# Five tiles of the third path block summed in PSUM instead of four, and two of the second block's tiles scattered at the border of the blocks

## What is computed

```python
x1 = x_nodes[src].reshape(-1, N_SEG, EXTENT)            # 4352 edges, 16 segments of 32
x2 = x_edges.reshape(-1, N_SEG, EXTENT)
i1, i2, i3 = (path_indices[:, 0], path_indices[:, 1], path_indices[:, 2])   # 64 paths
contrib = path_coeffs[None, :, None] * x1[:, i1, :] * x2[:, i2, :]
edge_out = jnp.zeros((x2.shape[0], N_SEG, EXTENT)).at[:, i3, :].add(contrib)
out = jnp.zeros((n_nodes, OP_SIZE)).at[dst].add(edge_out.reshape(-1, OP_SIZE))
```

## Time and profile before

| | |
|---|---|
| median of 3 runs | 277.52 us (277.49 to 278.12) |
| span of the profiled execution, first to last instruction | 276.2 us |
| PE busy | 263.4 us, 95% |
| DVE busy | 224.0 us, 81% |
| ACT busy | 164.3 us, 59% |
| block 2's paths on PE | 188.0 to 227.6 us |

### The profile page before, as it was taken

The page is one execution under the profiler, slowest core; times in us unless marked ns, Lnnn a source line. Parts: engine busy times, 40 slices in busy tenths (PEclk is TensorE's granted clock), DMA queues, the critical chain, the costliest instruction groups (busy, mean ns, idle before and its releaser), DMA issues.

```text
span 276.2 us, 5644 instructions
## 1 busy us (share of the span) xinstructions
PE 263.4 (95%) x1631; PEld 185.6 (67%) x1639; DVE 224.0 (81%) x660; ACT 164.3 (59%) x335; POOL 63.1 (23%) x52
## 2 busy tenths in 40 slices
PE   6899999999999899998999999969999999999996
PEld 4566698886444799996678776746656674468633
DVE  5977565199657999999999999999999987655372
ACT  6920551011526699946879786497898839352260
POOL 4000060060006644304769991000000000000000
PEclk9999999999999999999999999977999999999999
DMA  6699990000014557733150002014445428100002
GB/s 203 232 414 405 447 397 12 0 2 1 1 38 129 177 144 252 233 100 101 53 139 17 2 1 76 4 37 141 148 154 152 154 84 320 54 2 2 2 0 76
DMA packets 12592, 33.91 MB, mean 123 GB/s; under 512 B 3345, under 2 KB 3602, under 8 KB 12306
## 3 DMA queue, kind: packets, MB, share of 16 engines
q1 hardware_dynamic: 10482, 26.73, 27.0%
q0 software_dynamic: 2080, 6.82, 8.4%
HBM read 32.50 MB, written 1.05 MB: 121 GB/s over the span
## 4 chain that ended last, share of the span: by engine, by line
PE 85%; DVE 7%; ACT 3%; issue 2%; POOL 1%; ACTq 0%; DVEq 0%; POOLq 0%
PE psum L1276 16%; PE psum L1327 16%; PE psum L1230 10%; PE psum L1330 8%; PE psum L1254 5%; PE psum L1259 4%; PE psum L1282 3%; PE psum L1401 3%; PE psum L1427 3%; PE psum L1173 3%; PE psum L1159 2%; PE psum L1318 2%; PE psum L1182 1%; PE psum L1439 1%; PE psum L1320 1%
## 5 line engine op out<-in xcount | busy, mean ns | idle before, releaser
L460 POOL DMA_INDIRECT big<-xn_rows,big x26 | 51.4, 1975 | 54.4 <-DMA xn_rows<-xn 23.5
L1276 PE MATMUL psum<-big,dst_oh 128*128 128x512 f32 x108 | 51.3, 601 | 0.0
L595 ACT ACTIVATE prod<-edges,coef_b 128x320 f32 (+1 forms) x77 | 42.6, 590 | 11.0 <-PE psum L1330 8.4
L1011 DVE TENSOR_TENSOR prod<-big,prod 128x320 f32<-128x320 f32 (+1 forms) x77 | 40.5, 528 | 0.4 <-DVE big L982 0.2
L1327 PE MATMUL psum<-prod,ident 128*128 128x128 f32 x160 | 31.8, 293 | 0.7 <-DVE prod L1011 0.5
L1327 PEld LDWEIGHTS psum<-prod,ident 128*128 128x128 f32 x160 | 24.5, 190 | 10.0 <-issue 9.2
L1276 PEld LDWEIGHTS psum<-big,dst_oh 128*128 128x128 f32 x108 | 19.1, 195 | 14.9 <-issue 14.9
L1230 PE MATMUL psum<-edges,big 128*128 128x256 f32 x128 | 28.3, 380 | 0.0
L1230 PEld LDWEIGHTS psum<-edges,big 128*128 128x128 f32 x128 | 24.1, 190 | 3.5 <-issue 0.3
L1021 DVE TENSOR_TENSOR big<-big,prod 128x64 f32 (+2 forms) x80 | 26.3, 329 | 0.1
L595 ACT ACTIVATE xparts<-edges,coef_b 128x320 f32 (+1 forms) x45 | 23.9, 582 | 0.9 <-PE psum L1327 0.8
(11 more groups left out here) (215 smaller groups left out, 491.6 us busy)
## 6 DMA issues: line engine op xcount, KB each, us to landing
big<-in_w SPq DMA_DIRECT2D x3, 2048.0 KB, 16.3
edges<-in_f SPq DMA_DIRECT2D x11, 512.0 KB, 3.5
edges<-in_edge SPq DMA_DIRECT2D x1, 3584.0 KB, 23.9
edges<-in_edge SPq DMA_DIRECT2D x1, 2560.0 KB, 23.5
edges<-in_edge SPq DMA_DIRECT2D x5, 512.0 KB
edges<-in_f SPq DMA_DIRECT2D x1, 2560.0 KB, 10.4
big<-in_gnn_w SPq DMA_DIRECT2D x1, 1024.0 KB, 6.2
xs<-in_x SPq DMA_DIRECT2D x1, 512.0 KB, 3.5
```

Of the source, the lines that this page charges most:

```text
L460: nc.gpsimd.indirect_dma_start(out=x1g[b % 2][:, i, :], out_offset=None, in_=xn_rows, in_offset=bass.IndirectOffsetOnAxis(ap=idx_i[:, 0, F ...
L595: nc.scalar.activation(slot(n)[:, 0:BLOCKS[b], :], segment(edges[:, FIRST[b]:FIRST[b] + BLOCKS[b], :], single_column(words, p)), ACT.Copy, ...
L1011: nc.vector.tensor_tensor(v, segment(xg[:, 0:tiles, :], first_column(words[b], p)), v, ALU.mult).then_inc(mults, 1)
L1276: last = mm(bank[2 + h], dst_oh[:, n % DR, h * P:(h + 1) * P], tile_sums(b, t), start=False, stop=False)
```

## The change

KEPT[2] becomes 5, and EARLY names 2 tiles of block 1 whose scatters stand ahead of the clearing of block 2's banks.

```diff
-    KEPT = [8, 6, 4]
+    KEPT = [8, 6, 5]
+    EARLY = [0, 0, 2]
...
         def scatter_paths(b):
-            n = BLOCKS[b - 1] if b else 0
-            return [1 + i * (NP - 4) // n for i in range(n)]
+            n = BLOCKS[b - 1] - EARLY[b] if b else 0
+            return [-1] * EARLY[b] + [1 + i * (NP - 4) // n for i in range(n)]
...
                     pe.wait_ge(gathered_odd, PE_TILES // 2)
+                for n, t in scatters[:EARLY[b]]:
+                    scatter(b - 1, n, t)
                 for i, q in enumerate(sum_banks(b)):
```

## The result

| | before | after |
|---|---|---|
| median | 277.67 us (277.49 to 278.12, 4 runs) | 289.65 us (289.57 to 289.67, 4 runs) |
| span of the profiled execution | 276.2 us | 287.8 us |
| PE busy | 263.4 us | 276.7 us |
| DVE busy | 224.0 us | 223.4 us |
| block 2's paths on PE | 188.0 to 227.6 us | 189.0 to 239.0 us |

The kernel is slower by 4.3%: the ratio is 1.0431 with an interval of 1.0418 to 1.0443. The forecast was 289.7, in a range of 286.5 to 293.5. The row of medians has all four runs of the kernel before, where the 277.52 that the prediction starts from has three.

A forecast was written before the change was run, and what follows sets the result against it. PE, without a gap in block 2 and matched with DVE to 0.3 us, was taken as the bound. Paths +16.1, scatters -3.4, clock -1.25 and later start +0.85 gave about 12.2 on 277.5: 289.7 us, range 286.5 to 293.5.

The forecast's parts named there:

- What bounds block 2: Before the change, PE and DVE are both full in block 2 and matched to within 0.3 us.
- Cannot take more work: In block 2, PE cannot take more work without a later end, whatever DVE saves.
- The price of a path on PE: Block 2: weight loads, not columns, set PE's pace; 0.475 us a path with the second matmul, paths +16.1 us in all.
- the rest for 31 fillers: Block 2's paths: of their 16.1 us growth, about 14.3 for 128 more instructions, the remainder for 31 fillers.
- The early scatters: Two scatters moved out of block 2 into PE's wait at the border: -3.4 us.
- The border: Between blocks 1 and 2: scatters fill PE's 2.09 us wait, clock stays at full speed, path 0 starts at 188.85.
- The rival in which the clock falls all the same: At the border before block 2, the clock still drops to 0.50: 3.6 us more, 293.3 us; chance 0.13.
- DVE and the tail: DVE's path in block 2 falls to 0.637 us, held back by slots; behind the paths nothing is exposed, the tail moves unchanged.
- The signs: Expected in the profile after: 32-column second-matmul rows starting 0.11 us apart, ACT waiting for PE's `psums` in nearly every path.
- The sum: Whole kernel: PE ends block 2's paths 12.2 us later, 277.5 + 12.2 = 289.7 us.
- Columns set the price: Block 2: narrow matmuls' loads hide under neighbours, a path takes 0.33 us; +3.1 us, 280.6 us; chance 0.08.
- Faster: Block 2: PE's added instructions go under DVE's cover and the end follows DVE, 2.2 us less, 275.3 us; chance 0.03.

The follow-up runs named there:

- the run with the clock alone: The kernel before with 20 bfloat16 matmuls of zeros (256 columns) ahead of block 2's clears, nothing else: 277.54 us, ratio 0.9991.

## Why the prediction was right

**What bounds block 2.** Both engines full and matched to 0.3 us was right of the profiled execution, and enough for the sign. That PE cannot take the fifth tile without a later end is shown by the run with the fifth tile alone. "Cannot take more work" was too strict: with its clock at 1.00 PE had room of about 1.9 us (40.2 - 38.3, the run with the clock alone), and 15 us did not fit. What I had left open is now shown: before the change DVE sets the end, since neither two scatters fewer on PE nor a fast clock at the border move the median.

**The price of a path on PE.** Forecast 0.475 us, measured 0.461; 16.1 us more for the paths forecast, 29.4 - 14.3 = 15.1 measured. The mechanism, a weight load for each float32 instruction and not the columns, held: loads of 128 columns of float32 weights start 0.112 us apart with 20, 32, 64 and 128 columns streamed. The 0.106 that I read for 20 columns is 1.70 over 16, but 16 loads have 15 spacings; the loads themselves, before the change, give (1.87 - 0.19) / 15 = 0.112:

```profile
34.33 1.87 PEld L1220 LDWEIGHTS psum<-edges 128*128 128x128 f32 x16
```

The mis-sized term is "the rest for 31 fillers", 1.8 us, which measured 0.97: behind a 32-column matmul a filler costs 0.03, behind one of 64 in block 1 it cost 0.95 - 0.89 = 0.06. The row of block 1 was the right one to take, but it was not of the same width, and the difference sat in the filler.

**The early scatters.** -3.4 us forecast, -3.2 measured between the two kernels with the fifth tile. They are worth that only because PE had become the bound; ahead of the change they are worth nothing.

**The border.** Path 0 at 188.85 forecast, 189.00 measured, with bank 0 in no one's way. The rival in which the clock falls all the same did not come in the four executions of the changed kernel, but it is real: with the same border it fell in 3 of the 13 executions of the kernel without a second matmul, and these took 1.7 to 2.0 us more than its 276.05. There path 0 came 1.7 us later. My 3.6 was twice that, since the clock came back after 3.4 us and not after 6.8; what it would cost in the changed kernel no run shows.

**DVE and the tail.** DVE's path of 0.637 us came as forecast (block 2's first adds of 160 columns are 0.64 apart), it was held back by the slots, and its last piece of the splits was over at 249.41, 2.2 us ahead of its use at about 251.6.

**The signs.** Two did not come as I wrote them. The 32-column rows start 0.03 us apart; it is their loads that are 0.11 apart. And ACT waits for `psums` 11 times in the block, not in nearly every path: about once for each of the 12 scatters, for up to 1.4 us.

**The sum.** The forecast was off by 0.05 us, and that is luck: two errors cancel. The block was forecast 51.0 us long and is 50.0, so the paths end at 239.00 and not 239.8, and the span is 287.8 and not 288.4. Against that, what lies around the span is 1.8 us and not 1.3. The 1.3 set the profiled execution's 276.2 beside runs at 277.5, of which it was not one. The groups of experiments hold 47 more executions of the kernel before with their mean clock. The 7 with a mean of 0.987 or 0.988, as in the profile, took 278.05 us or more. Of the 40 with 0.994 to 1.00, 31 took 277.38 to 277.53. So about half as much time at the slow clock (0.994) costs the usual execution nothing, and the 1.25 us that I subtracted for it belong to the profiled execution. A single profiled execution at 276.2 beside runs at 277.5 should have made me ask whether it was one of them.

**The rivals.** "Columns set the price" is refuted by 289.65 where it had 280.6, and by the run with 128 columns (292.08 and not 300). "Faster" names a true bound, DVE: with PE's price taken away the change gives 1.4 us. It failed at the price, 0.24 us a path where 0.06 was the limit, as forecast.

No run here beats the kernel before with the whole computation in place. Summing all five tiles in one matmul of 160 columns would need one load less, but a segment of 160 columns does not divide a bank of 512 and the banks are not adjacent; that was not tried.

## What to carry to other kernels

Work that is moved from an engine to another has to be priced in the other engine's unit: here DVE's unit is a column (1 ns) and PE's is a float32 weight load (0.11 us), so 32 columns that cost DVE 0.033 us cost PE 0.223. A matmul whose weights are loaded anew is worth it only when it is wide; the same second matmul with four tiles' columns took 2.4 us more in the whole kernel, all of it in the fillers.

Where two engines are matched, take load off each of them alone before you believe that one is the bound: the same two scatters were worth nothing in one kernel and 3.2 us in the other. And compare the profiled execution's span with those of the other runs before you subtract anything that only it shows.

## What the runs showed of the hardware

Weight loads of 128 float32 columns start 0.112 us apart, whether 20, 32, 64 or 128 columns are streamed behind them, and loads of 64 columns 0.055 apart (the run with half the weights). At 512 columns the stream is longer than the load: one scatter, four instructions, takes 1.72 us.

A change of the weights' width between two matmuls is dear. Going from 128 columns of weights to 64 put 0.205 us between the starts, and back to 128 0.152, where two neighbours of 128 are 0.112 apart and the two narrow ones 0.079; with two changes in each path the kernel lost 12.6 us although every narrow load was shorter (132 ns instead of 190).

Behind a bfloat16 load of 128 columns the next load started 0.028 us later, a quarter of the 0.112 behind a float32 one, and its record is 98 to 100 ns long instead of 190. The Trainium skill (TensorE: Matmul & The Clock Gate, Weight-path perf modes — Fast Weight Load (FWL) and DoubleRow) has a fast load for weights of 128 columns that are not FP32; the run agrees, with these numbers. The first of two such loads behind a wide float32 matmul gained nothing: the second came 0.11 us after it.

At the border PE stood idle for only 0.26 us between the last path of block 1 and the early scatters. The granted clock still fell in 3 of 13 executions of the kernel without a second matmul; two of them were traced, and there it went to 0.50 at 183.5, just after the scatters had begun, for 3.4 us. It fell in none of the 34 executions of the other six kernels with the same queue up to there. What decides it stays open.
